# Router logits with tokens as the stationary side, unrolled loops, and work moved into gaps, in an attention and expert kernel

## The reference

```
x = x + tanh(g_xattn) * (attention(layernorm(x), ctx; 16 heads of 64) @ Wo + bo)
h = layernorm(x)
gates  = softmax(h @ router_w)                      # 14 experts
masked = top 2 of gates, divided by their sum
ffn(e) = silu((h / rms(h) * rms_w[e]) @ W1[e]) @ W2[e]      # 256 -> 512 -> 256
x = x + tanh(g_ffn) * (sum over e of masked[:, e] * ffn(e) + two shared ffn)
```

## Time and profile before

| what | value |
|---|---|
| median of three runs | 1460.05 us |
| the profiled execution's own time | 1458.97 us |
| its span (first to last instruction) | 1457.2 us |
| granted TensorE clock, mean | 0.999 |
| PE busy | 1435.2 us (98%), 9774 matmuls |
| PE weight loads busy | 1346.5 us (92%) |
| DVE busy | 1081.7 us (74%) |
| ACT busy | 935.1 us (64%) |
| POOL busy | 463.4 us (32%) |

### The profile page before, as it was taken

How to read it: one execution, slowest core, us unless ns; L and a number is a source line. 1 busy time by engine, 2 the same in 40 slices (tenths; PEclk the granted TensorE clock), 3 DMA queues, 4 the chain that set the end, 5 groups by cost and what they waited for, 6 DMA issues and landing times.

```text
span 1457.2 us, 31992 instructions
## 1 busy us (share of the span) xinstructions
PE 1435.2 (98%) x9774; PEld 1346.5 (92%) x9774; DVE 1081.7 (74%) x2614; ACT 935.1 (64%) x2398; POOL 463.4 (32%) x688
## 2 busy tenths in 40 slices
PE   7999999999999999999999999999999999999998
PEld 7999999999999999999999999998789978888888
DVE  4878888888888888888788888878587444444448
ACT  6777777777776777777777777776453345455452
POOL 4313142231323413143231332417100145555520
PEclk9999999999999999999999999999999999999999
DMA  4010311213112131211303112150022346662235
GB/s 125 7 51 17 115 74 51 95 31 114 76 49 79 50 108 38 93 74 55 107 15 116 74 49 85 44 191 32 28 102 116 142 168 237 213 236 85 78 130 213
DMA packets 55583, 137.07 MB, mean 94 GB/s; under 512 B 10496, under 2 KB 38160, under 8 KB 51920
## 3 DMA queue, kind: packets, MB, share of 16 engines
q1 hardware_dynamic: 48880, 118.01, 23.4%
q0 software_dynamic: 6624, 18.13, 3.9%
HBM read 86.69 MB, written 49.43 MB: 93 GB/s over the span
## 4 chain that ended last, share of the span: by engine, by line
PE 95%; DVE 2%; ACT 1%; issue 1%; DMA 0%; SPq 0%; ACTq 0%; DVEq 0%
PE bank L586 19%; PE bank L587 18%; PE bank L588 18%; PE bank L647 10%; PE bank L1702 7%; PE bank L1045 6%; PE bank L1037 5%; PE bank L1722 4%; PE bank L1726 2%; PE bank L1712 2%; PE bank L1689 1%; PE bank L1218 1%; PE bank L602 1%; DVE pT_lo L855 1%; DVE nmax L872 0%
## 5 line engine op out<-in xcount | busy, mean ns | idle before, releaser
L763 ACT ACTIVATE prob<-bank,nmax 128x375 f32<-128x375 f32 x448 | 258.8, 578 | 190.3 <-DVE nmax L872 188.3
L855 DVE TENSOR_TENSOR pT_lo<-bank,pT_hi 125x384 fp32r<-125x384 f32 x448 | 246.2, 550 | 25.3 <-ACT pT_hi L774 23.7
L872 DVE TENSOR_REDUCE nmax<-bank 128x1 f32<-128x375 f32 x448 | 241.3, 539 | 29.9 <-PE bank L588 28.6
L647 PE MATMUL bank<-keep_ident,prob 128*125 128x128 f32 x1344 | 221.0, 273 | 0.9 <-DVE prob L881 0.9
L774 ACT CAST pT_hi<-bank 125x384 fp32r<-125x384 f32 x448 | 212.6, 475 | 1.7 <-PE bank L647 1.7
L647 PEld LDWEIGHTS bank<-keep_ident,prob 128*125 128x125 f32 x1344 | 201.4, 187 | 6.9 <-DVE prob L881 1.2
L586 PE MATMUL bank<-attend_wvo_hi,zT_hi 128*112 128x256 f32 x512 | 169.4, 331 | 0.7 <-DVE x L916 0.7
L586 PE MATMUL bank<-pT_hi,kv_hi 125*128 125x448 f32 x384 | 152.8, 398 | 4.3 <-DVE zT_lo L855 1.6
L586 PE MATMUL bank<-attend_kvT_hi,qp_hi 128*128 128x376 f32 x448 | 152.0, 339 | 1.4 <-ACT prob L763 1.3
L587 PE MATMUL bank<-attend_kvT_hi,qp_lo 128*128 128x376 f32 x448 | 149.8, 334 | 0.0
L588 PE MATMUL bank<-attend_kvT_lo,qp_hi 128*128 128x376 f32 x448 | 149.0, 333 | 0.0
(11 more groups left out here) (238 smaller groups left out, 3724.8 us busy)
## 6 DMA issues: line engine op xcount, KB each, us to landing
w_split<-we_split SPq DMA_DIRECT2D x14, 2048.0 KB, 6.9
keep_weights<-w_split SPq DMA_DIRECT2D x14, 2048.0 KB
we_in<-in_w SPq DMA_DIRECT2D x28, 512.0 KB, 5.9
keep_y_all<-y_rows SPq DMA_DIRECT2D x14, 512.0 KB, 9.1
kv_in<-in_ctx SPq DMA_DIRECT2D x32, 187.5 KB
h_rows<-hrow SPq DMA_DIRECT2D x32, 112.4 KB, 2.3
keep_h_in<-h_rows SPq DMA_DIRECT2D x7, 514.0 KB, 9.3
x_in<-in_x SPq DMA_DIRECT2D x16, 224.0 KB, 2.8
```

Of the source, the lines that this page charges most:

```text
L647: last = nc.tensor.transpose(turn_bank_of(s)[0:MP, c * P:(c + 1) * P], prob[:, s % NB, c * MP:(c + 1) * MP], ident[:])
L763: nc.scalar.activation(prob[:, s % NB, :], score_bank(s)[:, 0:M], ACT.Exp, bias=nmax[:, s % NB:s % NB + 1], accum_out=psum_[:, s % NB:s % ...
L855: return nc.vector.tensor_tensor(dst, src, hi.bitcast(F32), ALU.subtract)
L872: nc.vector.tensor_reduce(nmax[:, s % NB:s % NB + 1], score_bank(s)[:, 0:M], AX, ALU.max, negate=True).then_inc(max_ready, 1)
```

## The change

It has seven parts.

1. The two transfers of the gates (`sync_gates`) are issued by ACT ahead of its tanh, no longer by SP ahead of everything else.
2. All loops over passes on PE, DVE, POOL and SP are written out.
3. In the last pass POOL runs `scale_shared` ahead of `ln2_root(29)` and of the last bias addition; `split_shared` stays behind both and so starts earlier too.
4. At the end of attention PE turns group 1 one step earlier.
5. The logits are formed with hT, 128 tokens, as the stationary operand and the router weight as the moving one: per group 4 blocks of tokens by 2 halves of D by 2 matmuls. The moving operand is hi and lo side by side (28 columns) for hT hi, and hi alone (14 columns) for hT lo. The result has tokens on the partitions; `copy_logits` and `turn_logits` go. `scale_logits` becomes three small DVE operations.
6. PE's first routed work (`turn_rows` of tiles 0 to 2, `hidden` of tiles 0 and 1) is put between the four parts of the last shared `output`; the routed stage swaps two pairs of PSUM banks.
7. The last group's store of `out` is issued in two halves.

```
-        def sync_gates(sp):
-            sp.dma_start(gates[:, 0:1], io["g_xattn"].partition_broadcast(P)).then_inc(gate_in, 16)
...
+        def sync_gates(act):
+            act.dma_start(gates[:, 0:1], io["g_xattn"].partition_broadcast(P)).then_inc(gate_in, 16)
...
-            body(0, FULL)
-            with eng.Fori(1, PAIRS - 1) as p:
-                body(p, FULL)
-            body(PAIRS - 1, LAST)
+            for p in range(PAIRS):
+                body(p, LAST if p == PAIRS - 1 else FULL)
...
-            with pool.Fori(1, PAIRS - 1) as p:
+            for p in range(1, PAIRS - 1):
                 body(p, False)
             p = PAIRS - 1
             split_context(p, 0)
             add_bias(p, 0)
             split_context(p, 1)
+            sb["scale_shared"](pool)
             ln2_root(2 * p - 1)
             add_bias(p, 1)
-            sb["scale_shared"](pool)
             pool.wait_ge(side_done, job_index(p, Q[7]) + 1)
...
             sb["turn"](pe, 0)
-            for s in range(last_tile(7) + 4, last_tile(7) + 6):
-                behind(last, s, (), True)
+            behind(last, last_tile(7) + 4, (), True)
             sb["turn"](pe, 1)
-            for s in range(last_tile(7) + 6, last_tile(7) + 9):
+            for s in range(last_tile(7) + 5, last_tile(7) + 9):
                 behind(last, s, (), True)
             sb["logits"](pe, 0)
...
-            for n, (k, (w, h)) in enumerate((k, q) for k in range(2) for q in PRODUCTS):
-                last = nc.tensor.matmul(lt_bank(g)[0:E, :], rwp[w][:, k, :], hT_of(sb, h, g)[:, k, :],
-                                        start=n == 0, stop=n == 5)
-            last.then_inc(lt_done, 1)
+            for t in range(4):
+                rows = slice(t * P, (t + 1) * P)
+                for k in range(2):
+                    nc.tensor.matmul(l_bank(g)[:, 2 * t * E:2 * (t + 1) * E], hT_of(sb, "hi", g)[:, k, rows],
+                                     rw_split[:, k, :, :].rearrange("p q e -> p (q e)"), start=t == 0 and k == 0,
+                                     stop=False, skip_group_check=True)
+                    last = nc.tensor.matmul(l_bank(g)[:, 2 * t * E:(2 * t + 1) * E], hT_of(sb, "lo", g)[:, k, rows],
+                                            rwp["hi"][:, k, :], start=False, stop=t == 3 and k == 1,
+                                            skip_group_check=True)
+            last.then_inc(l_done, 1)
...
                 if g < GROUPS:
                     logits(pe, g - 1)
-                turn_logits(g - 2)
+            pe.wait_ge(l_ready, GROUPS - 2)
...
+                nc.vector.tensor_tensor(here, parts[:, :, 0, :], inv, ALU.mult).then_inc(l_sum, 1)
+                nc.vector.tensor_tensor(weighed_lo[:, g % 2], parts[:, :, 1, :], inv, ALU.mult).then_inc(l_sum, 1)
+                dve.wait_ge(l_sum, 2 * g + 2)
+                nc.vector.tensor_tensor(here, here, weighed_lo[:, g % 2], ALU.add).then_inc(l_ready, 1)
...
             pe.wait_ge(silu_done, 4 * len(items))
-            sb["turn_first_rows"](pe)
-            output(len(items) - 1)
+            sb["turn_rows"](pe, 0)
+            output(len(items) - 1, (0,))
+            sb["turn_rows"](pe, 1)
+            output(len(items) - 1, (1,))
+            sb["routed_hidden"](pe, 0)
+            output(len(items) - 1, (2,))
+            sb["routed_hidden"](pe, 1)
+            sb["turn_rows"](pe, 2)
+            output(len(items) - 1, (3,))
...
-            sb["split_first_rows"](dve)
-            for t in range(4):
+            sb["split_rows"](dve, 0)
+            sb["split_rows"](dve, 1)
+            for t in (0, 1):
+                accumulate(len(items) - 1, t)
+            sb["split_rows"](dve, 2)
+            for t in (2, 3):
                 accumulate(len(items) - 1, t)
...
-        HT_BANK, H_BANK, T_BANK, O_BANK = banks[0:2], banks[2:4], banks[4:6], banks[6:8]
+        HT_BANK, H_BANK, T_BANK, O_BANK = banks[0:2], banks[2:4], banks[6:8], banks[4:6]
...
+            g = GROUPS - 1
+            for t in (0, 2):
+                sp.wait_ge(acc_done, 4 * (g - BEFORE) + t + 2)
+                sp.dma_start(by_group(io["out"], g)[:, t:t + 2, :], acc[:, 4 * g + t:4 * g + t + 2, :]).then_inc(out_stored, 16)
```

More of the change, by code:

```diff
@@ L431, in store @@
                 sp.dma_start(io["h_rows"][bass.ds(bi * N, N)], hrow[:, b, :]).then_inc(h_stored[b], 16)
-            weights["sync_gates"](sp)
             load_x(0)
@@ L469, in sync @@
             body(0, FULL)
-            with sp.Fori(1, PAIRS - 2) as p:
+            for p in range(1, PAIRS - 2):
                 body(p, FULL)
@@ L792, in ln2_roots @@
                 nc.scalar.activation(rs2[:, 2, :], rs2[:, 1, :], ACT.Exp, scale=-0.5).then_inc(ln2_act, 1)
+            weights["sync_gates"](act)
             weights["tanh"](act)
@@ L1066, in front @@
         rw = buf("rw", [P, 2, E])
-        rwp = {q: buf("rw_" + q, [P, 2, E], F32R) for q in ("hi", "lo")}
-        logitT, logit, prob, tie, scan1 = sb["logitT"], sb["logit"], sb["gate_prob"], sb["tie"], sb["scan1"]
+        rw_split = buf("rw_split", [P, 2, 2, E], F32R)
+        rwp = {q: rw_split[:, :, i, :] for i, q in enumerate(("hi", "lo"))}
+        logit, prob, tie, scan1 = sb["logit"], sb["gate_prob"], sb["tie"], sb["scan1"]
+        weighed_lo = sb["weighed_lo"]
         both, pos, scan = tie, prob, [logit, scan1]
@@ L1249, in hidden, with output @@
                     shared_hidden(nc, sb, g, e, j, H_BANK[j]).then_inc(h_done, 1)
-            def output(i):
+            def output(i, parts=range(4)):
                 e = items[i][1]
                 pe.wait_ge(hid_lo_ok, 4 * i + 4)
-                for t in range(4):
+                for t in parts:
                     if e == 0 and items[i][0] > 0 and t % 2 == 0:
@@ L1691, in turn_rows, with part, hidden @@
             last.then_inc(h_turned, 1)
-        def tensor(pe):
-            def part(slot, at, n):
-                return weights[:, bass.ds(slot, 1), at:at + n].rearrange("p s n -> p (s n)")
-            def hidden(t, slot):
-                b = t % 2
-                pe.wait_ge(hT_lo, t + 1)
-                for k in range(2):
-                    for q, (a, at) in enumerate((("hi", 0), ("lo", 0), ("hi", HID))):
-                        last = nc.tensor.matmul(H_BANK[b][:, :], hT[a][:, b, k, :], part(slot, 2 * k * HID + at, HID),
-                                                start=k == 0 and q == 0, stop=k == 1 and q == 2)
-                last.then_inc(hid_done, 1)
+        slots = {}
+        def part(slot, at, n):
+            return weights[:, bass.ds(slot, 1), at:at + n].rearrange("p s n -> p (s n)")
+        def hidden(pe, t):
+            b = t % 2
+            slot = slots[t] = pe.value_load(ring_of[0:1, t:t + 1], min_val=0, max_val=RING - 1)
+            pe.wait_ge(hT_lo, t + 1)
+            for k in range(2):
+                for q, (a, at) in enumerate((("hi", 0), ("lo", 0), ("hi", HID))):
+                    last = nc.tensor.matmul(H_BANK[b][:, :], hT[a][:, b, k, :], part(slot, 2 * k * HID + at, HID),
+                                            start=k == 0 and q == 0, stop=k == 1 and q == 2)
+            last.then_inc(hid_done, 1)
+        def tensor(pe):
             def turn_hidden(t):
@@ L1730, in tensor @@
             pe.nop(nofuse=True).then_inc(o_done, 1)
-            slots = {}
-            for t in range(SLOT_TILES + 2):
-                if t < SLOT_TILES:
-                    slots[t] = pe.value_load(ring_of[0:1, t:t + 1], min_val=0, max_val=RING - 1)
-                    hidden(t, slots[t])
-                if t + 1 < SLOT_TILES:
+            for t in range(1, SLOT_TILES + 2):
+                if 2 <= t < SLOT_TILES:
+                    hidden(pe, t)
+                if 3 <= t + 1 < SLOT_TILES:
                     turn_rows(pe, t + 1)
-                if 1 <= t <= SLOT_TILES:
+                if t <= SLOT_TILES:
                     turn_hidden(t - 1)
@@ L1772, in scalar @@
             rows_hi(0)
+            rows_hi(1)
             for t in range(SLOT_TILES + 2):
```

55 lines of the change are left out of this document (15 added, 40 removed).

## The result

The changed kernel takes 1475.62 us, the kernel before in the same series 1460.01; the ratio is 1.0104 with a 95% interval of 1.0091 to 1.0117. It is 15.6 us slower where 5 us less were forecast. The profiled execution has a span of 1473.7 us, 16.4 more than before.

What follows compares the result with a forecast made beforehand. PE was taken as the bound, 95% of the chain's span. Terms -0.9 - 1.0 - 0.5 - 0.9 - 0.6 - 1.3 = -5.2 took 1458.97 to 1453.8, plus 1.08 to 1454.9 us; range 1451.9 to 1458.4.

Steps and rivals of the forecast that it cites:

- routed begin: Start of the routed stage: PE's waits of 1.34 and 0.91 go, a new one of about 1.0 comes; -1.3 us.
- three signs of being wrong: Passes shorter by more than 0.15, logit matmuls closer than 0.1, or PE losing over 4.4 in the last 44 us.
- POOL's order: Last pass of attention: two old waits go, -2.0, new meetings of POOL and DVE cost +1.5; -0.5 us in all.
- the two old waits: Last pass: DVE divisions at 1010.29 and 1014.87 delayed beside POOL's splits by 1.11 and 0.98; their going was put at -2.0.
- Logits: Router logits: 112 matmuls at 0.109 take 12.2 us instead of 12.77, only the copy's wait goes; -0.6.
- The bound of +0.7: Upper bound of the logits term, with the new matmuls at 0.120 us each.
- Loops: Loops over passes written out: 0.07 us saved up to step 13 in each of 14 passes; -1.0 in all.
- the second half: Rest of each pass, without a pair to compare: taken at nothing; if it gave as much again, loops would be -2.0.
- the second rival: Written-out loops also remove the wait that POOL's split causes in each pass: -3.0 more, 1451.9 us; chance 0.09.
- The slower rival: PE's written-out code must be fetched and PE runs dry each pass; at 0.6 us a pass 1463.3; chance 0.06.
- Group 1 turned earlier: End of attention: eight transposes fill PE's wait of 1.02 for DVE's zT_lo; -0.9 us, between 0 and -1.0.
- Gates: Kernel start: with ACT issuing the gates, SP issues Wk 0.92 earlier and PE starts earlier; -0.9 us, bounds 0 and -1.4.

Runs made afterwards that it cites:

- the parts together: Kernel before with loops written out, group 1 turned earlier, new routed begin and last store in halves: 1453.97 us against 1458.96, ratio 0.9963.
- the 488 trials: Four separate kernels, not computing the reference, starting one DVE division at varied moments of a GpSimd row; the longest division took 2.64 us.

## Why the prediction was wrong

**The sum.** -5.2 was forecast, +15.6 measured. The single parts add up: loops -4.2, order +11.4, logits +11.2, routed begin -0.7 (trace -1.3), gates 0, group 1 earlier -0.9 (between the last score and the last projection, loops alone against the parts together: 0.02 and -0.86), in all +16.8, where each term has an interval of one to four microseconds. The traces give the loops -3.8 and the order +10.3, so 15.6 is within what the parts add up to.

Two of the three signs of being wrong that the prediction names came true: the passes got shorter by more than 0.15 (0.30), and PE lost more than 4.4 in the last 44 us before the last projection (11.3).

**POOL's order** is the step that failed first: -0.5 forecast, +11.4 measured. Its upper bound was that "each meeting costs the rest of a POOL operation, up to 2.4". That DVE is shut out while GpSimd works was right, and the two old waits did go; but even without the hold their -2.0 was used up by new meetings (1454.0 against 1453.97). And one meeting cost eight operations. The rows of before, and each trial since, show DVE getting in at one of the next two ends, or beside the scaling at once; the prediction took that for a law, and it is not. The Trainium skill (SBUF — State Buffer, on the shared port pair) has the lock held for the instruction of whichever came first; the 488 trials agree with it for the split, and the five held divisions do not. What makes them so is open. Known is: it is always the division of step 16 of the last pass, started under the first or second CAST of a row that follows `add_bias` at once. Ruled out are the loops (the hold is there with them), a lack of nops, the queued row write, and what the four separate kernels copy.

**Logits.** The term of -0.6 was mis-sized by 11.8. The pace was right: 0.11 at full clock, against the 0.081 for 128 columns of the Trainium skill (TensorE: Matmul & The Clock Gate, "Back-to-back issue gap"), and the wait for the copy went. The bound of +0.7 had no room for what came. Two things were left out. The step that reads "only the wait goes" overlooked who gives a bank back: with two banks, `logits(2)` needs the first `scale_logits`, which stands behind all of attention's work on DVE, a wait of 1.43 for one of 0.47. And the price of a matmul was taken at full clock; after the change PE works about 20 us at 1.2 GHz. By the trace of the kernel with the logits alone, 10.1 us are lost from pass 15 to the first shared output product; at half clock 20 us can cost up to 10, so the clock is most of it (an estimate).

**Loops.** -1.0 forecast, -4.2 measured (-3.8 in the trace). The 0.07 up to step 13 was exact (29.06 in the loop, 28.98 to 28.99 written out). The term that was taken at nothing is the second half: 0.05 behind the score of step 15, and 0.16 to 0.17 around the wait at step 22, the second rival, which was priced at -3.0 more and given 0.09. The reason against it, that the start of GpSimd's split is at its place in the pass as before, was wrong: it starts 43.1 us behind the pass's first score instead of 43.4. The slower rival, written-out code that has to be fetched in every pass, did not occur: no pass got longer.

**Group 1 turned earlier** -0.9, **routed begin** -1.3: as forecast, by the traces. **Store in halves**: forecast 0; it was not put alone, and from the third routed tile to the end the changed kernel moves by under 0.1. The two waits of the earlier trace rows are gone and the new one is there, PE and DVE of the changed kernel:

```profile
1189.06 0.41 PE L1707 MATMUL bank<-keep_ident,keep_silu 128*128 128x128 f32 x2 [0.94 <-DVE keep_acc L1547]
```

```profile
1188.16 0.76 DVE L1547 TENSOR_TENSOR keep_acc<-bank,keep_acc 128x256 f32<-128x256 f32 x2 [0.25 <-PE bank L1040]
```

**Gates.** -0.9 forecast, 0 measured, which was the bound "Wk's landing is held by something else".

## What to carry to other kernels

Before a dense row of GpSimd operations is moved, list which SBUF-to-SBUF operations of DVE it will meet, and take as the upper bound the whole row, not one operation; a wait that lets the critical one pass first took the loss away here (1454.0 with it, 1465 without), though the new order then gained nothing over the old. Do not thin out matmuls for their own sake: fewer columns with a new stationary operand each bought no time at 0.11 apiece, and half the clock for 20 us. When a buffer is done away with, look up who releases the one that takes its place. And change such parts one at a time: here parts worth -6 and parts worth +22 went in together.

## What the runs showed of the hardware

- A DVE division from SBUF to SBUF was held over eight back-to-back GpSimd operations (12.34 to 12.75 us in three kernels here and in the changed one), and over a row of four in one more (6.19), while the same pair in kernels of its own never took over 2.64. Cause open.
- The granted clock fell to half with PE without a gap, under 128x128 transposes and matmuls of 14 to 28 columns, and in that stretch returned only with 512-column matmuls.
- With two small broadcast loads moved to a second queue, the next big load was issued 0.92 earlier and landed at the same moment (5.2 us behind its issue instead of 4.3), and the operation that needs the small ones started at 6.67 instead of 3.99. What held them is open.
- Writing loops out shortened 13 of 14 passes by 0.30, of which 0.07 up to step 13, and one by 0.02.
